# Relation-aware graph attention on one core: Q evicted by VectorE behind the sort, the one-hot cut by tile, gathers that begin before the edge phase is declared ready

## The chip, the core and the metric

The kernel runs on one core of a Trainium2 chip. The core has five engines with a program each: TensorE (PE in the profile; PEld is its weight load), VectorE (DVE), ScalarE (ACT), GpSimd (POOL) and SyncE (SP). They meet at semaphores. DMAs are issued by SP, ACT and POOL and run on 16 shared DMA engines; an indirect DMA (a gather of rows by an index column) is issued by GpSimd. The metric is device time in microseconds, lower is better.

## What is computed

Five relations, four heads of 64, N = 6250 nodes of 256 features, E = 100000 edges with a source, a destination and a relation each:

```python
Q = (jnp.einsum('nc,rch->rnh', x, Wq) + bq[:, None, :]).reshape(R, N, HEADS, OUT)
K = (jnp.einsum('nc,rch->rnh', x, Wk) + bk[:, None, :]).reshape(R, N, HEADS, OUT)
V = (jnp.einsum('nc,rch->rnh', x, Wv) + bv[:, None, :]).reshape(R, N, HEADS, OUT)
q_i = Q[edge_type, dst]
k_j = K[edge_type, src]
v_j = V[edge_type, src]
score = jnp.sum(q_i * k_j, axis=-1) * scale
seg = dst * R + edge_type
m = jax.ops.segment_max(score, seg, num_segments=N * R)
e = jnp.exp(score - m[seg])
s = jax.ops.segment_sum(e, seg, num_segments=N * R)
alpha = e / s[seg]
out = jax.ops.segment_sum(v_j * alpha[..., None], dst, num_segments=N)
...
x = _layernorm(x + out.reshape(N, HD) + bias, axis=-1)
```

Everything is float32. The edges are drawn at random and come unsorted.

## The kernel before

**Stage 1, projections and sort, side by side.** The nodes are 49 tiles of 128 rows (the last has 106). TensorE goes through 392 *chunks* (`for o in range(NO)`): first 147 chunks of Q, three per tile (512, 512 and 256 columns), then 245 of K and V, five per tile of 512 columns. A chunk is two matmuls, one per half of the 256 features; each fp32 matmul appears in the trace as two records. In a Q chunk a bf16 matmul with three rows (L544) puts the bias into the bank first. Chunk `o` uses bank `o % 4`, so it waits until chunk `o - 4` is evicted. ScalarE evicts all chunks below `OA` with a copy (L684), VectorE those from `OA` on with an addition of the bias (L967); before, `OA = NOQ = 147`, so VectorE evicts K and V. After chunk 0 of each Q tile TensorE transposes the next tile of x (L486). SP stores each finished Q tile to `q_tab` (L440), ScalarE's queue stores each K/V tile to `kv_tab` (L693).

Meanwhile VectorE sorts the edges by destination and relation with a bitonic network on a 128 x 1024 array of keys: 322 min/max entries of 512 columns (L855). Some layers need the array turned: TensorE transposes it (`turn_keys`, L498) and either VectorE reads it with a change of sign ("toT"), or ScalarE copies both halves back to SBUF (L715, "toR"); seven turns each way, and a last one. The places of the turns between chunks, `turn_at`, come from a small table of costs in units of one sort entry; `OS` is the first chunk behind the sort, 113 before. Then VectorE runs index steps 0 to 3 (`indices(step)`, L873 to L891), which give `kvidx` and, last, `qidx`; from chunk `OS` on it runs one step per chunk, each behind that chunk's eviction, if it has one (steps 4 to 14, `Z = OS - 4`).

With `qidx` there, GpSimd gathers 391 tiles of 128 query rows ahead of need (L373) into a ring of 14 slots `pq`, and SP stores them in order of use to `q_pre` (L431). Gather `j` below 49 needs the first `j + 1` tiles of Q in `q_tab`. SP's `keep_queries` comes four to a tile from tile `first = (OS + 2) // 3` on. From j = 72 on a gather also waits for a count of K/V evictions.

**Stage 2, edges.** 832 edge tiles of 128 edges, in 208 *superblocks* of four. GpSimd gathers K/V rows (L390) into a ring of 14 superblocks, and the 441 query tiles that were not prepared (L395); SP loads the 391 others from `q_pre` (L454). ScalarE lifts the queries to PSUM (L767), VectorE multiplies and reduces to scores (L987, L989), a softmax over segments follows once in eight superblocks, ScalarE scales V (L778), and 11 superblocks later TensorE sums by destination with a one-hot matrix (L608) that VectorE builds (L1036), and VectorE adds into `acc` (L1049). Before it all, `s_ready` must be given by VectorE (L981), which waits until everything of stage 1 is done, for the two stages share one region of SBUF.

**Stage 3** joins chunk borders, adds x and bias, and normalizes.

GpSimd's order between stage 1 and 2 is fixed by hand:

```python
pool.wait_ge(s_kvout[0], 16 * (NT // 2 + 2))
pool.wait_ge(s_kvout[1], 16 * (NT // 2))
pool.wait_ge(s_ready, 1)
for s in range(NSB):
```

## Time and profile before

| | us |
|---|---|
| median of 3 runs (lowest, highest) | 2569.26 (2567.68, 2575.88) |
| the profiled execution, its own time | 2567.08 |
| its span in the trace | 2565.3 |
| busy: TensorE / VectorE / ScalarE / GpSimd | 1631.4 / 1672.7 / 1222.1 / 1649.2 |

The profile page gives each engine's busy time, the span in 40 slices, the chain of work that ended last and the costliest groups of instructions. The groups have busy time, mean time of one, and the idle time of the engine just before them with what ended it; "issue" there means that nothing in the profile was waited for. The timeline lists instructions by start. Ends of matmuls are modelled. The granted TensorE clock is 1.00 up to 760 us and 0.5 to 0.7 from there on.

### The profile page before, as it was taken

How to read it: one execution, taken by the hardware profiler on the slowest of the kernel's cores; microseconds unless marked ns; L12 is line 12 of the kernel's file. 1: busy time of each engine (PE TensorE's matmuls, PEld its weight loads, DVE VectorE, ACT ScalarE, POOL GpSimd, SP SyncE). 2: the span in 40 equal slices, each digit the busy share in tenths (PEclk: the TensorE clock that was granted, in tenths of full speed). 3: DMA queues.
4: the chain of work that ended last, by engine and by line, in shares of the span. 5: the costliest groups of instructions: out<-in, count | busy, mean ns of one | idle time of the engine just before them, and what ended most of it. 6: DMA issues, size and time to landing. Idle time of an engine off the chain costs nothing.

```text
span 2565.3 us, 26061 instructions
## 1 busy us (share of the span) xinstructions
PE 1631.4 (64%) x5906; PEld 1128.7 (44%) x5906; DVE 1672.7 (65%) x3127; ACT 1222.1 (48%) x4159; POOL 1649.2 (64%) x1745
## 2 busy tenths in 40 slices
PE   7999999999990455545555555555544555555547
PEld 2444444444440344444444444444444444444435
DVE  8888333443435767777767777777767777777658
ACT  2333310000001666666666666666666666666656
POOL 1000557777776777777777777777777777777404
PEclk9999999999995555666665656666666566565675
DMA  5333789999998766666666666666666666666305
GB/s 185 123 117 117 245 292 363 363 362 364 363 360 295 222 195 200 195 197 200 199 198 199 197 200 199 198 199 199 197 196 199 197 199 201 199 199 199 109 11 174
DMA packets 285621, 553.28 MB, mean 216 GB/s; under 512 B 43605, under 2 KB 167719, under 8 KB 285466
## 3 DMA queue, kind: packets, MB, share of 16 engines
q0 software_dynamic: 106496, 327.26, 42.6%
q1 hardware_dynamic: 142836, 156.41, 18.4%
q10 hardware_dynamic: 36134, 67.94, 7.5%
q8 instruction: 48, 0.79, 0.1%
q14 instruction: 107, 0.88, 0.1%
HBM read 397.78 MB, written 153.65 MB: 215 GB/s over the span
## 4 chain that ended last, share of the span: by engine, by line
POOL 35%; PE 26%; issue 19%; ACT 7%; DVE 6%; DMA 6%; SPq 0%; DVEq 0%; POOLq 0%; ACTq 0%
POOL region L390 24%; PE sums L547 20%; POOL region L395 11%; ACT region L778 6%; DMA region<-q_tab,qidx 4%; PE sums L608 3%; DVE region L855 3%; PE sums L544 1%; DMA q_pre<-region 1%; DVE region L1127 1%; DVE region L1130 1%; ACT pairs L767 0%; DMA region<-kv_tab,kvidx 0%; POOL region L373 0%; DVE acc L1116 0%
## 5 line engine op out<-in xcount | busy, mean ns | idle before, releaser
L608 PE MATMUL sums<-region 128*128 128x130 f32 x3328 | 783.3, 420 | 787.3 <-ACT region L778 755.4
L608 PEld LDWEIGHTS sums<-region 128*128 128x128 f32 x3328 | 712.6, 320 | 845.0 <-ACT region L778 842.5
L390 POOL DMA_INDIRECT region<-kv_tab,kvidx x832 | 808.2, 971 | 261.9 <-issue 242.8
L778 ACT ACTIVATE region<-region 128x64 f32<-128x64 f32 x3328 | 821.5, 333 | 0.0
L547 PE MATMUL sums<-region,acc 128*128 128x512 f32 (+2 forms) x1568 | 673.7, 577 | 0.9 <-DVE region L967 0.9
L373 POOL DMA_INDIRECT region<-q_tab,qidx x391 | 371.9, 951 | 390.4 <-DVE qidx L891 249.8
L767 ACT COPY pairs<-region 128x1024 f32<-128x1024 f32 x208 | 211.4, 1016 | 792.4 <-DMA region<-kv_tab,kvidx 473.9
L1049 DVE TENSOR_TENSOR acc<-acc,sums 128x256 f32 x832 | 349.3, 420 | 327.9 <-PE sums L608 257.0
L395 POOL DMA_INDIRECT region<-q_tab,qidx x441 | 423.4, 960 | 134.4 <-issue 131.9
L547 PEld LDWEIGHTS sums<-region,acc 128*128 128x128 f32 (+1 forms) x1568 | 285.8, 190 | 314.1 <-issue 303.1
L967 DVE TENSOR_TENSOR region<-sums,region 128x512 f32<-128x512 f32 (+1 forms) x245 | 169.1, 691 | 301.0 <-PE sums L547 298.1
L987 DVE TENSOR_TENSOR pairs<-region,pairs 128x1024 f32<-128x1024 f32 x208 | 253.2, 1217 | 31.2 <-ACT pairs L767 31.0
L989 DVE TENSOR_REDUCE region<-pairs 128x16 f32<-128x1024 f32 x208 | 255.0, 1226 | 7.1
L855 DVE TENSOR_TENSOR region<-region 128x512 f32<-128x512 f32 x306 | 198.0, 689 | 19.6 <-ACT region L715 14.5
L684 ACT COPY region<-sums 128x512 f32<-128x512 f32 (+1 forms) x147 | 75.6, 514 | 213.9 <-PE sums L547 213.9
L1036 DVE TENSOR_TENSOR region<-iota_f,nrel 128x520 f32<-128x520 f32 x208 | 144.3, 694 | 0.0
L404 POOL TENSOR_TENSOR region<-region 128x256 f32<-128x256 f32 (+1 forms) x49 | 35.4, 729 | 117.8 <-DMA region<-in_x 117.6
L993 DVE TENSOR_TENSOR_SCAN region<-PEN,region 128x128 f32<-128x128 bf16 x52 | 24.2, 464 | 89.0 <-ACT region L750 70.5
L655 PE MATMUL sums<-ident,acc 128*128 128x128 f32 (+1 forms) x196 | 54.3, 435 | 27.8 <-DVE acc L1116 18.5
L729 ACT COPY region<-bank 1x512 f32<-1x512 f32 x52 | 29.4, 566 | 78.1 <-PE bank L568 78.1
L655 PEld LDWEIGHTS sums<-ident,acc 128*128 128x128 f32 (+1 forms) x196 | 42.3, 305 | 39.6 <-DVE region L1127 21.0
L544 PE MATMUL sums<-region 3*128 3x512 bf16 (+1 forms) x147 | 51.5, 350 | 9.0 <-DMA region<-region 9.0
(187 smaller groups left out, 783.0 us busy)
## 6 DMA issues: line engine op xcount, KB each, us to landing
kv_tab<-region ACTq DMA_DIRECT2D x48, 1280.0 KB, 7.5
q_pre<-region SPq DMA_DIRECT2D x391, 128.0 KB, 5.1
region<-q_pre SPq DMA_DIRECT2D x391, 128.0 KB, 3.5
q_tab<-region SPq DMA_DIRECT2D x48, 640.0 KB, 3.2
region<-q_tab,qidx POOLq DMA_INDIRECT x832, 3.7
region<-kv_tab,kvidx POOLq DMA_INDIRECT x832, 3.6
region<-in_x SPq DMA_DIRECT2D x96, 128.0 KB, 3.1
out<-region SPq DMA_DIRECT2D x48, 128.0 KB, 1.8
```

The lines of the kernel that those rows point to most:

```text
L373: pool.indirect_dma_start(pq[:, j % PQ, :], None, q_tab[0:min(stored * P, N) * R, :], bass.IndirectOffsetOnAxis(ap=qidx[:, PRE[j]:PRE[j] + ...
L390: pool.indirect_dma_start(ring[:, s % KS, i, :], None, kv_tab, bass.IndirectOffsetOnAxis(ap=kvidx[:, t:t + 1], axis=0)).then_inc(s_got[s % ...
L395: pool.indirect_dma_start(qring[:, s % QS, i, :], None, q_tab, bass.IndirectOffsetOnAxis(ap=qidx[:, t:t + 1], axis=0)).then_inc(s_got[s % ...
L547: done = nc.tensor.matmul(bank[o % 4][0:n, 0:w], acc[:, k, t * P:t * P + n], w_sb[:, k, :, :].rearrange("p u c -> p (u c)")[:, c0:c0 + w], ...
L608: done = nc.tensor.matmul(bank[i][:, h * W:(h + 1) * W], ring[:, q % KS, i, h * P:(h + 1) * P], oneh[:, q % 2, i, :], start=True, stop=True)
L767: nc.scalar.copy(qk, qring[:, s % QS, :, :]).then_inc(s_lift, 1)
L778: done = nc.scalar.activation(ring[:, q % KS, i, h * D:(h + 1) * D], ring[:, q % KS, i, C + h * D:C + (h + 1) * D], ACT.Copy, scale=alT[:, ...
L855: nc.vector.tensor_tensor(to[:, :, half, :], a[:, :, half, :], other_half, ALU.max if half else ALU.min).then_inc(s_sort, 1)
L967: nc.vector.tensor_tensor(stage[0:n, t % 2, c0:c0 + w], bank[o % 4][0:n, 0:w], b_sb[0:n, c0:c0 + w], ALU.add).then_inc(s_evD, 1)
L987: c(nc.vector.tensor_tensor(qk, ring[:, s % KS, :, 0:C], qk, ALU.mult))
L989: nc.vector.tensor_reduce(sc[:, (s // PERC) % 2, :, g:g + SB].rearrange("p h g -> p g h"), qk.rearrange("p i (h d) -> p i h d", h=H), AX.X ...
L1049: nc.vector.tensor_tensor(acc[:, :, bass.ds(at[i], P)], acc[:, :, bass.ds(at[i], P)], bank[i][:, 0:2 * W].rearrange("p (h n) -> p h n", h= ...
```

## The change

**Sort.** In a toR turn TensorE transposes the upper half first; ScalarE copies only that half, and VectorE's next two sort entries read the lower half from PSUM. The table of places counts nothing more for a toR turn; `OS` becomes 111, and most turns from the seventh on move one to two chunks forward.

**Queries first.** Index step 0 computes `qidx` in four operations, straight from the keys; what else steps 0 to 3 gave comes after it.

**Q evictions.** `OA` becomes 114: the chunks of Q tiles 38 to 48 (33 chunks) have no bias matmul, and VectorE evicts them with an addition of the bias row, held in `bq_sb`, which five more DMAs fill at the start.

**Handover.** GpSimd waits for `s_ready` only at superblock 3 (`FIRST`), since the first three ring slots lie where the weights were. The last K/V tile is stored relation by relation.

**One-hot.** Four `tensor_scalar` of 130 columns with a scalar column in place of one `tensor_tensor` of 520.

```diff
-                sort_at = turned + (2.5 if kind == "toR" else 0)
+                sort_at = turned
...
-    OA = NOQ
+    OA = QC * (OS // QC + 1)
...
+        bq_sb = stage[:, 1, 0:R * C]
...
+        FIRST = KC * UNITS * C // (SB * 2 * C)
...
-            return max(0, (j - EASE) * (NO - NOQ) // NPRE)
+            done = (j - EASE) * (NO - NOQ) // NPRE
+            return NOQ - OA + done if done > 0 else 0
...
-            pool.wait_ge(s_kvout[0], 16 * (NT // 2 + 2))
+            pool.wait_ge(s_kvout[0], 16 * (NT // 2 + 2 * R))
             pool.wait_ge(s_kvout[1], 16 * (NT // 2))
-            pool.wait_ge(s_ready, 1)
             for s in range(NSB):
+                if s == FIRST:
+
+                    pool.wait_ge(s_ready, 1)
...
+            for q in range(R):
+                sp.dma_start(bq_sb[:, q * C:(q + 1) * C], bq[q:q + 1, :].broadcast_to([P, C])).then_inc(s_bq, 16)
...
-                for half in range(2):
+                for half in (1, 0) if kind == "toR" else (0, 1):
...
-                    for half in range(2):
-                        act.wait_ge(s_turn, 2 * m + half + 1)
-                        nc.scalar.copy(keys[1 - TURNS[m][2]][:, half * 512:(half + 1) * 512], bank[5 + half][:]
-                                       ).then_inc(s_back, 1)
+                    act.wait_ge(s_turn, 2 * m + 1)
+                    nc.scalar.copy(keys[1 - TURNS[m][2]][:, 512:1024], bank[6][:]).then_inc(s_back, 1)
...
+            for r in range(R):
+                wait_evicted(act, NO - R + r)
+                for lo, hi in parts(NT - 1):
+                    act.dma_start(kv_rows[(NT - 1) * P + lo:(NT - 1) * P + hi, r, :],
+                                  stage[lo:hi, (NT - 1) % 2, r * CH:(r + 1) * CH]).then_inc(s_kvout[(NT - 1) % 2], 16)
...
+                    if back:
+
+                        dve.wait_ge(s_turn, 2 * back[0] + 2)
+                        dve.wait_ge(s_back, len([m for m in TURNS[0:back[0] + 1] if m[1] == "toR"]))
+                        one, other_half = bank[5][:].unsqueeze(1), a[:, :, 1, :]
...
+                    c.go(nc.vector.tensor_scalar(real[:], two[:, 0:TT, 0], float(DUMMY), None, ALU.is_lt))
...
+                    c(nc.vector.scalar_tensor_tensor(out=nrel[:], in0=two[:, 0:TT, 1], scalar=float(R - 8), in1=segi[:],
+                                                     op0=ALU.mult, op1=ALU.add))
+                    nc.vector.scalar_tensor_tensor(out=qidx[:], in0=nrel[:], scalar=float((8 - R) * HI), in1=real[:],
+                                                   op0=ALU.add, op1=ALU.mult).then_inc(s_qready, 1)
...
+                if OA <= o < NOQ:
+                    if o % QC == 0:
+                        dve.wait_ge(s_qout[t % 2], 16 * (t // 2))
+                    dve.wait_ge(s_proj, o + 1)
+                    q0 = c0 - 2 * R * C
+                    nc.vector.tensor_tensor(stage_q[0:n, t % 2, q0:q0 + w], bank[o % 4][0:n, 0:w],
+                                            bq_sb[0:n, q0:q0 + w], ALU.add).then_inc(s_evD, 1)
...
-                nc.vector.tensor_tensor(oneh[:, q % 2, :, :], iota_f[:].unsqueeze(1).broadcast_to([P, SB, W]),
-                                        nrel[:, q * SB:(q + 1) * SB].unsqueeze(2).broadcast_to([P, SB, W]),
-                                        ALU.is_equal).then_inc(s_oh, 1)
+                for i in range(SB):
+                    t = q * SB + i
+                    done = nc.vector.tensor_scalar(oneh[:, q % 2, i, :], iota_f[:], nrel[:, t:t + 1], None, ALU.is_equal)
+                done.then_inc(s_oh, 1)
```

On TensorE, behind the cast of index rows in Q tile 37 or 38 (L504 to L508 before, L514 to L518 in the change). Before:

```order
L505 MATMUL bank<-region 128x320
L508 MATMUL bank<-region 128x26 x4
L544 MATMUL sums<-region 128x512
L547 MATMUL sums<-region,acc 128x512 x2
L544 MATMUL sums<-region 128x256
L547 MATMUL sums<-region,acc 128x256 x2
L544 MATMUL sums<-region 128x512
L547 MATMUL sums<-region,acc 128x512 x2
L486 MATMUL pairs<-ident,region 128x128 x2
```

In the change:

```order
L515 MATMUL bank<-region 128x320
L518 MATMUL bank<-region 128x26 x4
L554 MATMUL sums<-region 128x256
L557 MATMUL sums<-region,acc 128x256 x2
L557 MATMUL sums<-region,acc 128x512 x2
L496 MATMUL pairs<-ident,region 128x128 x2
L557 MATMUL sums<-region,acc 128x512 x2
L525 MATMUL pairs<-region 128x512
```

The cast stands two chunks earlier in the program, and the one chunk after it is the last with a bias matmul (L554); before, all 147 had one.

On VectorE, from the cast's results on (L902 before, L922 in the change; `region` is most of SBUF). Before:

```order
L902 SCALAR_TENSOR_TENSOR region<-pairs,region 128x512 [waits s_cast,s_dve]
L904 SCALAR_TENSOR_TENSOR region<-bank,region 128x320
L908 TENSOR_SCALAR reci<-bank 1x52
L910 COPY recS<-bank 128x2x26
L916 TENSOR_TENSOR region<-region,recS 128x832 [waits s_dve,s_castc]
L917 TENSOR_TENSOR region<-region 128x832 [waits s_dve]
L920 TENSOR_TENSOR region<-region,recS 128x832 [waits s_dve]
L921 TENSOR_TENSOR region<-region 128x832 [waits s_dve]
```

In the change:

```order
L989 TENSOR_TENSOR region<-sums,region 128x512 [waits s_proj,s_qout0,s_dve]
L922 SCALAR_TENSOR_TENSOR region<-pairs,region 128x512 [waits s_cast]
L924 SCALAR_TENSOR_TENSOR region<-bank,region 128x320
L928 TENSOR_SCALAR reci<-bank 1x52
L930 COPY recS<-bank 128x2x26
L989 TENSOR_TENSOR region<-sums,region 128x512 [waits s_proj,s_dve,s_castc]
L936 TENSOR_TENSOR region<-region,recS 128x832
L937 TENSOR_TENSOR region<-region 128x832 [waits s_dve]
L989 TENSOR_TENSOR region<-sums,region 128x256 [waits s_proj,s_dve]
L940 TENSOR_TENSOR region<-region,recS 128x832
L941 TENSOR_TENSOR region<-region 128x832 [waits s_dve]
```

An eviction of a Q chunk (L989) now stands ahead of each index step.

On GpSimd, from the last query gather on (L373 and L390 before, L379 and L398 in the change). Before:

```order
L373 DMA region<-q_tab,qidx 128x256 [waits s_pqout12,s_evicted_dve]
L390 DMA region<-kv_tab,kvidx 128x512 [waits s_ready,s_kvout1,s_kvout0]
L390 DMA region<-kv_tab,kvidx 128x512 x11
L390 DMA region<-kv_tab,kvidx 128x512 [waits s_lifted]
L390 DMA region<-kv_tab,kvidx 128x512 x3
```

In the change:

```order
L379 DMA region<-q_tab,qidx 128x256 [waits s_pqout12,s_evicted_dve]
L398 DMA region<-kv_tab,kvidx 128x512 [waits s_kvout1,s_kvout0]
L398 DMA region<-kv_tab,kvidx 128x512 x11
L398 DMA region<-kv_tab,kvidx 128x512 [waits s_lifted,s_ready]
L398 DMA region<-kv_tab,kvidx 128x512 x3
```

The wait for `s_ready` has moved back by 12 gathers.

## Rows read from the trace of the kernel before

**Rows 1.** The page: its head, DMA busy in tenths by 40 slices, the chain by engine

```profile
span 2565.3 us, 26061 instructions
...
DMA  5333789999998766666666666666666666666305
...
POOL 35%; PE 26%; issue 19%; ACT 7%; DVE 6%; DMA 6%; SPq 0%; DVEq 0%; POOLq 0%; ACTq 0%
```

**Rows 2.** Groups, GpSimd, 783 to 2410 us: busy, mean of one | idle before

```profile
L390 POOL DMA_INDIRECT region<-kv_tab,kvidx x832 | 808.2, 971 | 261.9 <-issue 242.8 <-PE sums L608 9.1 <-DVE region L981 8.7
L395 POOL DMA_INDIRECT region<-q_tab,qidx x441 | 423.4, 960 | 134.4 <-issue 131.9 <-ACT pairs L767 2.4
```

**Rows 3.** Timeline, handover from query to K/V gathers: start, us, engine, line, operation

```profile
774.25 0.94 POOL L373 DMA_INDIRECT region<-q_tab,qidx  x1 [0.30 <-issue]
782.52 0.49 DVE L980 MEMSET region<- 1x516 f32 x1 [16.63 <-DMA q_pre<-region]
...
783.91 0.95 POOL L390 DMA_INDIRECT region<-kv_tab,kvidx  x1 [8.71 <-DVE region L981]
...
793.23 1.02 ACT L767 COPY pairs<-region 128x1024 f32<-128x1024 f32 x1 [448.01 <-DMA region<-kv_tab,kvidx]
```

**Rows 4.** Timeline, GpSimd, the last gather

```profile
2402.12 0.95 POOL L395 DMA_INDIRECT region<-q_tab,qidx  x1 [0.30 <-issue]
```

**Rows 5.** Timeline, GpSimd: gather 19, and the 48th and 49th query gathers

```profile
289.97 0.94 POOL L373 DMA_INDIRECT region<-q_tab,qidx  x1 [2.74 <-DMA q_pre<-region]
...
339.84 0.94 POOL L373 DMA_INDIRECT region<-q_tab,qidx  x1 [4.00 <-DMA q_tab<-region]
346.78 0.94 POOL L373 DMA_INDIRECT region<-q_tab,qidx  x1 [6.00 <-DMA q_tab<-region]
```

**Rows 6.** Timeline, TensorE: a Q tile's bias matmul to the next tile's, then K/V

```profile
239.69 0.38 PE L544 MATMUL sums<-region 3*128 3x512 bf16 x1
...
245.65 0.38 PE L544 MATMUL sums<-region 3*128 3x512 bf16 x1
...
739.68 25.48 PE L547 MATMUL sums<-region,acc 128*128 128x512 f32 x59
```

**Rows 7.** Timeline, VectorE's first and last operation for qidx, the first gather

```profile
254.18 0.59 DVE L874 CAST region<-region 128x832 f32<-128x832 uint16 x1
...
261.38 1.02 DVE L891 TENSOR_TENSOR qidx<-nrel,region 128x832 int32<-128x832 f32 x1
...
262.69 1.36 POOL L373 DMA_INDIRECT region<-q_tab,qidx  x1 [249.81 <-DVE qidx L891]
```

**Rows 8.** Timeline, the seventh toR turn; then VectorE's waits, 0 to 262 us

```profile
236.22 0.66 PE L498 MATMUL pairs<-ident,region 128*128 128x128 f32 x4 [0.80 <-DVE region L855]
...
236.91 0.58 ACT L715 COPY region<-pairs 128x512 f32<-128x512 f32 x1 [1.08 <-PE pairs L498]
...
238.09 3.35 DVE L855 TENSOR_TENSOR region<-region 128x512 f32<-128x512 f32 x5 [1.92 <-ACT region L715]
...
DVE region L855 <- ACT region L715: 14.5, 7, 2.8
```

**Rows 9.** Timeline, VectorE and GpSimd where they meet; L1008 alone; L841 alone

```profile
849.04 0.69 DVE L1036 TENSOR_TENSOR region<-iota_f,nrel 128x520 f32<-128x520 f32 x1
849.19 1.36 POOL L390 DMA_INDIRECT region<-kv_tab,kvidx  x1 [0.30 <-issue]
...
285.81 0.59 DVE L941 TENSOR_SCALAR nrel<-nrel 128x832 f32<-128x832 f32 x1
285.98 1.25 POOL L373 DMA_INDIRECT region<-q_tab,qidx  x1 [0.30 <-issue]
...
830.11 0.95 POOL L390 DMA_INDIRECT region<-kv_tab,kvidx  x1 [0.30 <-issue]
830.74 0.34 DVE L1008 TENSOR_SCALAR PEN<-XF 128x129 bf16<-128x129 bf16 x1
...
16.08 0.75 DVE L841 TENSOR_SCALAR region<-region 128x1024 f32<-128x1024 f32 x1
```

More of the change, by code:

```diff
@@ L117, in gnn_kernel @@
             OS = o
-    OA = NOQ
+    OA = QC * (OS // QC + 1)
     Z = OS - 4
-    assert OS < NOQ and Z + 15 + NCK + 4 < NO, Z
+    assert OA < NOQ and Z + 15 + NCK + 4 < NO, Z
     ctx = ExitStack()
@@ L196, in gnn_kernel @@
         ring = cut(KS * SB * 2 * C).rearrange("p (s i w) -> p s i w", s=KS, i=SB)
+        FIRST = KC * UNITS * C // (SB * 2 * C)
+        assert all(AHEAD[s] == SB for s in range(FIRST))
         qring = cut(QS * SB * C).rearrange("p (s i w) -> p s i w", s=QS, i=SB)
@@ L847, in sort_entry @@
                     dve.wait_ge(s_sort, e)
-                    dve.wait_ge(s_back, 2 * len([m for m in TURNS if m[1] == "toR" and m[0] <= e]))
                 if kind in ("flip", "half"):
@@ L887, in indices @@
                 if step == 3:
-                    c.go(nc.vector.tensor_tensor(kvidx[:], lof[:], real[:], ALU.mult))
-                    c(nc.vector.scalar_tensor_tensor(out=nrel[:], in0=nodef[:], scalar=float(R), in1=nrel[:],
-                                                     op0=ALU.mult, op1=ALU.add))
-                    nc.vector.tensor_tensor(qidx[:], nrel[:], real[:], ALU.mult).then_inc(s_qready, 1)
-                    dve.wait_ge(s_qready, 1)
+                    c(nc.vector.tensor_tensor(kvidx[:], lof[:], real[:], ALU.mult))
                 if step == 4:
```

25 lines of the change are left out of this document (13 added, 12 removed).

## The prediction

> **What bounds the kernel now.** I read the page's head and chain first, then GpSimd's groups and waits, then the timeline at the places where one stage hands over to the next. The chain that ended last [rows 1] is led by GpSimd's gathers (L390 and L395, 35%), and its "issue" share is the gap between them. In the edge phase GpSimd issues 832 + 441 = 1273 gathers without a real wait: the groups [rows 2] give 971 and 960 ns each, and the idle time before them, 261.9 + 134.4 us, is 0.30 us per gather but for some 14 us, 8.7 of them one wait for L981 at the very start. From the first at 783.91 [rows 3] to the last at 2402.12 [rows 4] that is 1618.2 us for 1272 pitches, 1.272 us each. An undisturbed gather takes 0.943 + 0.30, nearly 1.25 us. Behind the last gather comes a tail (2402 to 2565) that the change does not touch in anything that paces it.
>
> So the end moves by what the first edge gather gains, plus what the pitch gains. Going back from 783.91: GpSimd has issued the 391 query gathers one by one up to 774.25; from the 49th, at 346.78, they run at 427.47/342 = 1.250 us with no further wait [rows 3, 5]. That 49th gather waited 6.00 us for q_tab (the one before it 4.00): it needs the last tile of Q. It follows that **the end of the Q projections sets the gather stream, and the stream sets the end.** TensorE's K and V work is nearly parallel to it: its last eviction is at 765 and four of its chunks take some 1.72 us each [rows 6] (59 matmul records of a quarter chunk in 25.48 us), 245 chunks.
>
> **Part 1, 33 Q chunks without bias matmuls (tiles 38 to 48).** A tile with biases takes 245.65 - 239.69 = 5.96 us [rows 6]. Without them two chunks of 512 and one of 256 cost at K and V's rate 2.5 x 1.727 = 4.32, and the two transposes of x some 0.35: 4.67 us. A tile gains 1.29 us, 11 tiles 14.2 us. The lower end is the bias matmuls' own pitch alone, 0.3 us twice and 0.2, or 0.83 x 11 = 9.1 us; I take the K and V rate, since those are the same instructions. VectorE now evicts these chunks (0.7 us for 512 columns) between the index steps. Steps 8 to 14 are about two operations of 832 elements at 1.02 us per chunk [rows 7], so it falls behind: some 13 us of steps plus 4.3 us of evictions against 7 chunks of 1.6 us. TensorE may be four chunks ahead, which nearly covers it; it then waits for the flags that ScalarE turns into heads. I charge 1.5 us (0 to 4). The sort's shifts of place move turns between chunks and conserve TensorE's work. Net: Q ends **12.5 us earlier** (7 to 16), and so do the 49th gather and all behind it, since nothing behind it waits. K and V's last eviction comes as much earlier, near 753.
>
> **Part 2, sort and query rows first.** In a turn back (toR) VectorE stands from 236.17 to 238.09, 1.92 us, while TensorE transposes twice and ScalarE copies twice [rows 8]; the seven cost 14.5 us in the waits. Now only the second half is copied, beside the other half's transposes, so VectorE can go on 0.57 us sooner, when the first copy's slot ends: 4.0 us. The later "toT" turns, placed some chunks sooner, lose their two long waits but get small ones. Replaying the chunk table with these prices puts the last turn 3.8 us earlier. Then qidx: before, from the first index operation at 254.18 to the first gather at 262.69, 8.5 us; now two of 0.59, two of 1.02 and the semaphore gaps, 3.6 us. So the first gather comes about 8.7 us earlier, near 254. I cost this at nothing: gathers 15 to 48 wait for the ring of 14 slots, which SP empties four to a tile [rows 5] (the 2.74 us), and the 48th and 49th for Q's last tiles. If that cover were gone it would be worth up to 8.7 us; it isn't, since 48 gathers need 60 us and Q's end is 80 us away.
>
> **Part 3, the handover.** After the last query gather at 774.25 GpSimd now waits only for the K/V stores, not for the landing, the store to q_pre and VectorE's clearing (782.52), so the next gather can follow at 1.25 instead of 9.66 us [rows 3]: **8.4 us**. The K/V stores are issued by then with 8 us to spare, and the last is cut into five. What is late next: gather 13 waits for s_ready and the first lift. Ready comes 8.9 us after the last query gather, gather 13 would go 16.3 us after it; the lift needs four loads issued after ready and took until 10.1 us behind it (793.23), but then it waited for its K/V rows. I expect it at 15, so this fits by a hair. Bounds: 8.4, or 4 if the lift is as late as it was.
>
> **Part 4, one-hot by tile.** The trace shows what the old operation does to GpSimd. L1036 starts at 849.04 and takes 0.69; the gather of 849.19 takes 1.36 instead of 0.94: it ends 0.82 after L1036 does [rows 9]. A compare of two SBUF operands holds a gather's beginning. Counted over the timeline, 109 of the 1273 gathers began under L1036, the first at 849.19, and together lost 23.7 us of the 31 that [rows 2] hold over 943 ns. A tensor_scalar in fp32 does it too: L941 of 285.81, and the gather of 285.98 takes 1.25, again 0.82 behind its end. The other way round, L1008 began 0.63 us into a gather and took 0.34 us instead of 0.20 [rows 9]: a scalar operation also meets the second half of a gather. So four short ones have two windows per gather, but each holds it for its own length only. Length: L841 with a scalar from SBUF takes 0.75 us for 1024, L941 0.59 for 832; columns cost 1.06 ns between L1036 (520, 0.69) and L891 (832, 1.02) and half of that in a scalar operation, so 130 columns come to 0.28 from L841 and 0.22 from L941, against 0.20 for L1008's 129: I take 0.25. Four in a row: 0.7 to 1.0 us in VectorE's superblock of 7.8 us, hidden, as VectorE is idle for over 2 us in each. Mean hold per superblock for random starts: before 0.69^2/2/1.27 = 0.19 us; now 4 x 0.25^2/2/1.27 = 0.10 in one window, up to 0.20 in both. That is 0 to 50% less than 23.7 us if the gather gets in between two of them. Bounds: all 24 us gained (no hold at all), or 25 us lost (the four act as one hold of 1 us in one window and a half). I take a gain of **2 us**.
>
> The Trainium skill (VectorE: DVE Perf Modes, "The TRN2 errata — SBUF-src ops pay a fixed extra latency per instruction") speaks against cutting one operation in four: a fixed cost is paid each time, and it advises 512 elements or more. By its formula four would take an estimated 0.51 us against 0.60 for one, as the halved rate pays for the fixed parts; the one took 0.69 here, and the four are not in this trace.
>
> **Sum** against the profiled execution's 2567.08 us: -12.5 - 8.4 - 2 = -22.9, so 2544.2. The median of the runs is 2.2 us higher: **2546.5**. A measurement here can tell 0.3%, 7.7 us, so faster means below 2561.5.
>
> **Rivals.**
> - *The one-hot gives its 24 us back whole* (10%): for it, that the scalar operand leaves VectorE's second read free; against it L941. 2524.
> - *The holds double* (16%): both windows are hit and the four act as one. Loss 15 to 25 us, time 2563 to 2572 at the far end, 2558 at the near one with a gain of Q at its upper bound. For it: operations without a wait between them follow at once.
> - *GpSimd is stopped by every scalar operation, wherever in the gather it falls* (5%). 832 operations x 0.25 us x 0.75 (a gather's share of its pitch) = 156 us more, less 23.7 and 21: 2680. It turns slower once a single operation costs GpSimd more than (21 + 24)/832 = 54 ns. For it: the first gather of all, which met two such operations and took 1.36 [rows 7]. Against it: L1008 lay within a gather of 0.95 us that was not longer [rows 9]. The Trainium skill (SBUF — State Buffer, "SBUF: two separate sides") states this rule: an operation in a 2-port mode takes the pair of ports as an exclusive lock, and GpSimd cannot write descriptors meanwhile; at a gather's beginning the trace agrees (0.82 us after the end, twice).
> - *Part 1 is eaten up* (9%): VectorE's evictions behind index steps hold TensorE for 8 us or more, Q ends 5 us earlier only: 2554.
> - *Nothing moves* (4%), because the transfers of the K/V phase, at nine tenths or more in all its slices [rows 1], pace the gathers and not their issue: against it the pitch of 1.250 us, the same as elsewhere.
>
> **Numbers.** Forecast as summed: 56%. The range 2525 to 2566 holds forecast, the eaten-up case, most of the first and of the doubled holds; outside stay the 5%, the far ends. Faster by over 0.3%: 0.85, within: 0.09, slower: 0.06.
>
> **What would show it.** First query gather near 254 and still waits of some us at the 48th and 49th, the 49th near 334; no wait after it; last one near 762; first K/V gather 1.25 us later; gather 13 with 0 to 2 us of wait; GpSimd's means near 0.965 in the edge phase; a tile of Q without biases at 4.7 to 5.3 us. I am wrong if the edge pitch is over 1.29 us, if K/V's last store lands after the last query gather, or if the tail behind the last gather changes from 163 us by more than 2.

## The result, and the profile after

The changed kernel takes 2540.77 us (median of 4 runs, 2539.55 to 2540.99), the kernel before 2572.17 in the same comparison (4 runs, 2567.68 to 2575.88): a ratio of 0.9865, 95% interval 0.9851 to 0.9878. The profiled execution took 2540.96 us against 2567.08, 26.1 us less. The forecast of 2546.5 was 5.7 us too high, its range held the time, and its sign was right. Its parts were not: two of the four terms were wrong by far, in opposite directions, as the traces show below.

The page of the changed kernel: head, DMA busy in tenths, the chain that ended last by engine (against [rows 1]).

```profile
span 2539.1 us, 26489 instructions
...
DMA  6333789999999766666666666666666666666305
...
POOL 33%; PE 26%; issue 16%; ACT 9%; DVE 9%; DMA 6%; SPq 0%; DVEq 0%; ACTq 0%; POOLq 0%
```

The groups of GpSimd and VectorE in the edge phase (against [rows 2]: 971 and 960 ns).

```profile
L398 POOL DMA_INDIRECT region<-kv_tab,kvidx x832 | 794.7, 955 | 255.3 <-issue 245.4 <-PE sums L618 7.0 <-ACT pairs L780 2.8
L403 POOL DMA_INDIRECT region<-q_tab,qidx x441 | 420.2, 953 | 134.5 <-issue 132.3 <-ACT pairs L780 2.1
...
L1066 DVE TENSOR_SCALAR region<-iota_f,nrel 128x130 f32<-128x130 f32 x832 | 186.2, 303 | 0.0
```

The timeline of the changed kernel at the places of [rows 3, 4, 5, 7]: start, us, engine, line, operation, idle before.

```profile
257.19 1.47 POOL L379 DMA_INDIRECT region<-q_tab,qidx  x1 [244.29 <-DMA q_tab<-region]
...
337.01 0.95 POOL L379 DMA_INDIRECT region<-q_tab,qidx  x1 [4.27 <-DMA q_tab<-region]
343.27 0.95 POOL L379 DMA_INDIRECT region<-q_tab,qidx  x1 [5.31 <-DMA q_tab<-region]
...
771.74 0.95 POOL L379 DMA_INDIRECT region<-q_tab,qidx  x1 [0.30 <-issue]
772.99 0.94 POOL L398 DMA_INDIRECT region<-kv_tab,kvidx  x1 [0.31 <-issue]
780.07 0.49 DVE L1008 MEMSET region<- 1x516 f32 x1 [18.72 <-DMA q_pre<-region]
787.84 1.02 ACT L780 COPY pairs<-region 128x1024 f32<-128x1024 f32 x1 [449.67 <-DMA region<-q_pre]
789.60 0.95 POOL L398 DMA_INDIRECT region<-kv_tab,kvidx  x1 [1.90 <-ACT pairs L780]
...
2376.36 0.95 POOL L403 DMA_INDIRECT region<-q_tab,qidx  x1 [0.30 <-issue]
```

Laid beside the rows of before, these marks divide the 26.1 us:

| stretch | before | after | difference | forecast |
|---|---|---|---|---|
| 49th query gather (end of Q) | 346.78 | 343.27 | -3.5 | -12.5 |
| 49th to last query gather | 427.47 | 428.47 | +1.0 | 0 |
| last query to first K/V gather | 9.66 | 1.25 | -8.4 | -8.4 |
| first to last gather of the edge phase | 1618.2 | 1603.4 | -14.8 | -2, and 0 to +2 at gather 13 |
| behind the last gather | 163.1 | 162.8 | -0.4 | 0 |

Q's end moved by a quarter of what was forecast, and the edge phase by seven times as much.

### The profile page after: what moved, and what is told of

Its sections match the earlier page's. It is cut to its first block, busy times and chain, and to the rows that moved or that the text cites. A ratio compares the mean times of both kernels' runs of the same rounds, so it can differ in the third digit from the quotient of the medians.

```text
span 2539.1 us, 26489 instructions
## 1 busy us (share of the span) xinstructions
PE 1619.8 (64%) x5873; PEld 1124.9 (44%) x5873; DVE 1729.1 (68%) x3784; ACT 1205.2 (47%) x4119; POOL 1633.8 (64%) x1745
## 4 chain that ended last, share of the span: by engine, by line
POOL 33%; PE 26%; issue 16%; ACT 9%; DVE 9%; DMA 6%; SPq 0%; DVEq 0%; ACTq 0%; POOLq 0%
POOL region L398 22%; PE sums L557 20%; POOL region L403 10%; ACT region L791 8%; DVE region L873 5%; DMA region<-q_tab,qidx 4%; PE sums L618 3%; DMA q_pre<-region 1%; ACT pairs L780 1%; PE sums L554 1%; DVE region L1156 1%; DVE region L1159 1%; DMA region<-in_x 0%; DVE acc L1078 0%; DVE acc L1145 0%
## 5 line engine op out<-in xcount | busy, mean ns | idle before, releaser
L398 POOL DMA_INDIRECT region<-kv_tab,kvidx x832 | 794.7, 955 | 255.3 <-issue 245.4
L379 POOL DMA_INDIRECT region<-q_tab,qidx x391 | 373.1, 954 | 386.7 <-DMA q_tab<-region 258.3
L873 DVE TENSOR_TENSOR region<-region 128x512 f32<-128x512 f32 x292 | 189.0, 689 | 5.1
L1066 DVE TENSOR_SCALAR region<-iota_f,nrel 128x130 f32<-128x130 f32 x832 | 186.2, 303 | 0.0
L694 ACT COPY region<-sums 128x512 f32<-128x512 f32 (+1 forms) x114 | 58.7, 515 | 181.4 <-PE sums L557 181.4
L598 PE MATMUL bank<-ident,region 128*128 128x128 f32 x26 | 11.0, 421 | 61.2 <-DVE region L1017 61.2
```

The source lines that it names most:

```text
L379: pool.indirect_dma_start(pq[:, j % PQ, :], None, q_tab[0:min(stored * P, N) * R, :], bass.IndirectOffsetOnAxis(ap=qidx[:, PRE[j]:PRE[j] + ...
L398: pool.indirect_dma_start(ring[:, s % KS, i, :], None, kv_tab, bass.IndirectOffsetOnAxis(ap=kvidx[:, t:t + 1], axis=0)).then_inc(s_got[s % ...
L873: nc.vector.tensor_tensor(to[:, :, half, :], one, other_half, ALU.max if half else ALU.min).then_inc(s_sort, 1)
L1066: done = nc.vector.tensor_scalar(oneh[:, q % 2, i, :], iota_f[:], nrel[:, t:t + 1], None, ALU.is_equal)
```

## The experiments

Three questions follow. Is the edge phase's gain the one-hot's, and is it the *kind* of operation (a scalar operand leaves VectorE's second read free) or the *length* of one operation that decides? Is Q's end late because VectorE's evictions lag behind the index steps (the rival "eaten up"), because of the heads' flags, which ride along with the same chunks, or because of TensorE's clock? And what is the handover worth once what comes behind it is counted? In the expectations "E" stands for the theory that TensorE's clock falls after its long standing idle before the first turn, and "G" for the theory that a slightly slower gather belongs to the chip and not to the program.

The marks of all traces, in us. "Idle" is TensorE's wait just before the first turn, "clock" what it was granted from 91 to 96 us, "held" the time by which the 1273 gathers of the edge phase exceed the median gather of their own trace, added up. That median is 949 ns in the changed kernel and 946 in the nine others, so 3.8 us of the changed kernel's edge phase are not in its "held". The four kernels of the last series are told of at their place.

| kernel | idle, clock | 49th query gather | last query gather | first K/V gather | last gather | edge phase | held |
|---|---|---|---|---|---|---|---|
| before | 1.41, 1.00 | 346.78 | 774.25 | 783.91 | 2402.12 | 1618.2 | 27.4 |
| changed | 2.27, 0.50 | 343.27 | 771.74 | 772.99 | 2376.36 | 1603.4 | 6.8 |
| e1_whole_onehot | 1.99, 0.66 | 341.86 | 769.42 | 771.03 | 2392.58 | 1621.5 | 29.1 |
| e2_only_onehot | 2.29, 0.50 | 350.20 | 777.82 | 788.24 | 2384.14 | 1595.9 | 5.1 |
| e3_onehot_tile_tt | 3.62, 0.66 | 342.26 | 769.84 | 771.09 | 2376.86 | 1605.8 | 12.3 |
| e4_ready_first | 1.89, 0.70 | 341.35 | 768.86 | 776.57 | 2373.56 | 1597.0 | 6.2 |
| e5_no_q_evict | 1.81, 1.00 | 347.08 | 774.56 | 775.81 | 2376.93 | 1601.1 | 7.0 |
| e6_late_flags | 2.83, 1.00 | 334.25 | 761.84 | 771.97 | 2368.79 | 1596.8 | 6.0 |
| e7_turn0_later | 0.99, 1.00 | 340.65 | 768.14 | 769.39 | 2370.05 | 1600.7 | 7.3 |
| e10_before_turn0 | 0.14, 1.00 | 347.80 | 775.36 | 785.49 | 2403.03 | 1617.5 | 26.8 |

The runs were made in series, each with runs of the kernel before beside it (the expectations call a series a "call"). Times are best compared within a series, as the kernel before itself had medians of 2572.17, 2569.11 (e1, e2, e3, e6) and 2569.27 us (e4, e5, e7, e10) in the three of this table. The changed kernel was in the first alone.

### e1_whole_onehot: all of the change but the one-hot

```diff
-                for i in range(SB):
-                    t = q * SB + i
-                    done = nc.vector.tensor_scalar(oneh[:, q % 2, i, :], iota_f[:], nrel[:, t:t + 1], None, ALU.is_equal)
-                done.then_inc(s_oh, 1)
+                nc.vector.tensor_tensor(oneh[:, q % 2, :, :], iota_f[:].unsqueeze(1).broadcast_to([P, SB, W]),
+                                        nrel[:, q * SB:(q + 1) * SB].unsqueeze(2).broadcast_to([P, SB, W]),
+                                        ALU.is_equal).then_inc(s_oh, 1)
```

> The changed kernel with the one-hot built by one tensor_tensor of 520 columns again. Theory A (short holds): a gather that begins under a VectorE operation waits for the end of that one operation only, so four operations of 0.28 us hold GpSimd far less than one of 0.69. Then the mean of an edge gather goes back from 955/953 ns to 971/960, the edge phase gets 15 to 17 us longer, and the time is 2556 to 2558. Rival B (the phase itself moved): the gathers became shorter because the edge phase starts in another rhythm, not because of the one-hot; then the means stay near 955 and the time stays within 3 us of 2541.

Measured: 2558.67 us (2555.11 to 2564.19), ratio to before 0.9962 (0.9951 to 0.9973). GpSimd's groups in the edge phase:

```profile
L398 POOL DMA_INDIRECT region<-kv_tab,kvidx x832 | 808.3, 972 | 255.4 <-issue 238.5 <-PE sums L618 12.8 <-ACT pairs L780 3.5
L403 POOL DMA_INDIRECT region<-q_tab,qidx x441 | 425.1, 964 | 134.3 <-issue 133.7 <-ACT pairs L780 0.6
```

The gathers are back at 972 and 964 ns, those of [rows 2], and the edge phase at 1621.5 us. The other three parts together are worth 0.4%; the greater part of the gain is the one-hot's.

### e2_only_onehot: the kernel before with the one-hot alone

The same edit the other way round, on the kernel before.

> The kernel before with the one-hot by tile alone. Theory A: 14 to 17 us faster than before, about 2555, with edge gathers at 953 to 956 ns. Rival B: within 3 us of before.

Measured: 2547.80 us (2546.79 to 2550.14), ratio 0.9918 (0.9902 to 0.9935).

```profile
L390 POOL DMA_INDIRECT region<-kv_tab,kvidx x832 | 790.9, 951 | 262.6 <-issue 242.8 <-DVE region L981 9.5 <-PE sums L608 7.9
L395 POOL DMA_INDIRECT region<-q_tab,qidx x441 | 418.4, 949 | 134.4 <-issue 132.5 <-ACT pairs L767 1.8
```

From 971 and 960 to 951 and 949 ns: the edge phase is 22.3 us shorter (1595.9 against 1618.2) with nothing else changed in it, and the time that gathers are held falls from 27.4 to 5.1 us. The expectation, read from the changed kernel's trace, had 14 to 17 us; the gain by the median is 21. The one-hot alone gives what e1 takes away (18.1 us, and the 3.8 of the median gather).

### e3_onehot_tile_tt: four short operations of the old kind

```diff
-                    done = nc.vector.tensor_scalar(oneh[:, q % 2, i, :], iota_f[:], nrel[:, t:t + 1], None, ALU.is_equal)
+                    done = nc.vector.tensor_tensor(oneh[:, q % 2, i, :], iota_f[:],
+                                                   nrel[:, t:t + 1].broadcast_to([P, W]), ALU.is_equal)
```

> The changed kernel with the one-hot by tile, but by four tensor_tensor of 130 columns instead of four tensor_scalar. If the length of the single operation decides, gathers keep 953 to 957 ns and the time stays within 2 us of the changed kernel (2541). If it is the kind (the scalar operand frees VectorE's second read), each of the four still holds like a quarter of the old one but they act as one hold of 0.7 to 1.0 us: gathers at 965 to 975 ns and 2553 to 2565.

Measured: 2541.41 us (2540.17 to 2541.89), ratio 0.9891 (0.9874 to 0.9907). The source view gives, for one line, min/median/max in ns, first and last start. In e3:

```profile
L1066 DVE TENSOR_TENSOR region<-iota_f,nrel x832: 256/286/355, 839.0 to 2437.3; 128x130 f32<-128x130 f32 x167
```

and in the changed kernel:

```profile
L1066 DVE TENSOR_SCALAR region<-iota_f,nrel x832: 252/281/520, 839.6 to 2436.4; 128x130 f32<-128x130 f32 x167
```

One operation takes 286 against 281 ns, and the mean gathers are nearly the same (957 and 953 ns against 955 and 953). But the changed kernel's median gather is the longer one. Held above their own median are 12.3 us in e3 and 5.1 to 7.3 in the six kernels of the table with the scalar form; e3's edge phase is 1605.8 us with 2.95 us at gather 13, that of e7 and e5 1600.7 and 1601.1 with 2.84 and 3.61. So most of the gain is the *length* of one operation (27.4 to 12.3, some 15 us), and the *kind* is worth some 5 us more, which the nearly equal run times hide. The expectation's two cases leave this one out. How the hold ends is seen in the changed kernel's timeline, VectorE and GpSimd:

```profile
839.57 0.87 DVE L1066 TENSOR_SCALAR region<-iota_f,nrel 128x130 f32<-128x130 f32 x4
...
839.85 1.01 POOL L398 DMA_INDIRECT region<-kv_tab,kvidx  x1 [0.31 <-issue]
```

The gather begins inside the row of four, which still has 0.59 us to go. By the rule of [rows 9], an end 0.82 us behind the operation's, it would have ended 1.41 us after its start had the four been one; it took 1.01, and its end is 0.82 us behind that of the second of the four (840.05). It was held by that one and got in ahead of the next. Counted from the starts and ends in the traces, 128 gathers began under the old one-hot and lost 23.4 us above the median (the forecast counted 109, and 23.7 us over 943 ns); under the four of the changed kernel 158 began and lost 2.4, under the four of e3 158, with 6.9. In all three the held ones end 0.81 to 0.83 us behind an operation.

In a gather's second half it is VectorE that waits: the short scalar operations that begin 0.50 to 0.60 us into a gather took mostly 500 down to 400 ns in place of 281, so that they end about 1.00 us behind the gather's start (the 520 ns above began at 0.48), and the gathers are not longer by it. Those that begin in its first 0.4 us are not slowed. The tensor_tensor form, at most 355 ns, is nearly free of that.

### e5_no_q_evict: the change with Q evicted as before

```diff
-    OA = QC * (OS // QC + 1)
+    OA = NOQ
```

> The changed kernel with OA = NOQ: ScalarE evicts all of Q again, and every Q chunk has its bias matmul; the half copy of the sort, the early qidx, the handover and the one-hot stay. Theory C: Q ends 6 to 8 us later (the 49th query gather at 349 to 351 instead of 343), the time is 2547 to 2549. By the prediction's own size of this part (12.5 us) it would be 2553; if K/V and not Q set the gather stream it would be within 2 us of 2541.

Measured: 2541.00 us (2538.96 to 2542.65), ratio 0.9889 (0.9872 to 0.9906). Its 49th gather starts at 347.08, that of before at 346.78 [rows 5]: the quicker sort and the earlier `qidx` give nothing at Q's end, so Part 2 is indeed covered. Against e7 below (340.65, the same granted clock) the 33 chunks are worth 6.4 us at the 49th gather, or 7.2 without the 0.8 us by which e7's own edit has Q late already at 245 us; between e2 (350.20) and the changed kernel (343.27), both at 0.50, 6.9 us. Forecast: 12.5. The expectation missed e5's time by 6 us (2547 to 2549): it was worked out from the changed kernel's trace, with its fallen clock and its gathers of 949 ns, and e5 has neither. In the same series e7 is 7.9 us below e5.

### e6_late_flags: the heads' flags moved behind Q

TensorE's flag transposes (L534, L535), ScalarE's copies and VectorE's last index steps move from chunks 120 to 145 into K and V's chunks, which have no bias matmul either.

```diff
+    X0 = NOQ
...
-                if Z + 13 <= o < Z + 13 + NCK:
-                    turn_same(o - Z - 13)
+                if X0 <= o < X0 + NCK:
+                    turn_same(o - X0)
...
-                indices(o - Z)
+                if o - Z < 15:
+                    indices(o - Z)
+                if o > X0 + NCK:
+                    indices(o - X0 + 13)
```

> The changed kernel with the 26 pairs of flag transposes (L534, L535) moved from the Q chunks 120 to 145 to the K/V chunks from 147 on. Theory C (why tiles of Q without bias gained 0.61 us and not 1.29): TensorE drains at every change between chunk matmuls and something else, and the flag transposes between the chunks keep that cost where the bias matmuls went. Then a Q tile without either takes 4.5 to 4.7 us instead of 5.88, Q ends 10 to 12 us earlier (the 49th query gather near 332 instead of 343), and since K/V then still ends where it did, 761, the last query gather (760) meets the K/V stores: the first K/V gather comes 5 to 9 us earlier and the time is 2532 to 2536. Rival D (VectorE's evictions pace the tiles): the tile stays over 5.3 us and the time within 3 us of 2541.

Measured: 2532.78 us (2529.37 to 2533.70), ratio 0.9854 (0.9838 to 0.9871): faster than the kernel before, and in the same series 8.6 us below e3, the change but for the one-hot's form. Against the changed kernel itself it isn't clear: 8.0 us by the medians of two series, but the ratios to before, 0.9854 and 0.9865, lie in each other's intervals. A tile of Q on TensorE, from one transpose of x to the next, first in the changed kernel:

```profile
311.81 0.38 PE L496 MATMUL pairs<-ident,region 128*128 128x128 f32 x2
312.03 0.27 PE L534 MATMUL pairs<-ident,region 128*128 128x128 f32 x1
312.23 0.22 PE L535 MATMUL pairs<-ident,region 1*128 1x1 f32 x1
312.38 1.98 PE L557 MATMUL sums<-region,acc 128*128 128x512 f32 x4
...
317.69 0.38 PE L496 MATMUL pairs<-ident,region 128*128 128x128 f32 x2
```

and in e6:

```profile
298.83 0.38 PE L497 MATMUL pairs<-ident,region 128*128 128x128 f32 x2
299.05 4.46 PE L558 MATMUL sums<-region,acc 128*128 128x512 f32 x12
303.35 0.38 PE L497 MATMUL pairs<-ident,region 128*128 128x128 f32 x2
```

5.88 us with flags, 4.52 without. The forecast had 4.67 for a tile without biases, near enough for a tile that nothing else interrupts. But 9 of the 11 tiles also carry flags, and a tile with biases *and* flags took 6.49 us in the kernel before: where the flags are, dropping the biases gains 0.61 us a tile and not 1.29. (That TensorE "drains" at such a change, as the expectation has it, no row shows; the rows show only the times.) Of the waits that the forecast had charged, the changed kernel's Q had two, 0.85 us for ScalarE at the first flag and 0.17 for VectorE.

That e6 has the 49th gather at 334.25, where the forecast had it "near 334", is in part chance, for its Q lost time in two other ways: TensorE stood 3.8 us for VectorE's evictions of Q, the longer time while VectorE itself waited 6.86 us for the store of an earlier Q tile, and behind that the granted clock was 0.50 for a while (waits; timeline of TensorE and VectorE; windows row, with 0.50 behind the five busy times).

```profile
PE sums L558 <- DVE region L990: 3.8, 2, 2.7
...
319.21 1.62 DVE L990 TENSOR_TENSOR region<-sums,region 128x512 f32<-128x512 f32 x3 [6.86 <-DMA q_tab<-region]
...
319.96 10.55 PE L558 MATMUL sums<-region,acc 128*128 128x512 f32 x24 [2.71 <-DVE region L990]
...
321.00:324.40 3.40, 3.40 (x8) 1.96 (x7) 1.29 (x2) 0.00 (x0) 2.48 (x4) 0.50 0.86 293
```

Of the 9.0 us that Q's end gains on the changed kernel, nearly all is lost again at the handover:

```profile
761.84 0.95 POOL L380 DMA_INDIRECT region<-q_tab,qidx  x1 [0.30 <-issue]
762.36 0.69 DVE L996 TENSOR_TENSOR region<-sums,region 106x512 f32<-106x512 f32 x1 [1.03 <-PE sums L558]
...
771.97 0.94 POOL L399 DMA_INDIRECT region<-kv_tab,kvidx  x1 [9.18 <-DMA kv_tab<-region]
```

The last eviction of K and V (762.36) now comes behind the last query gather (761.84), and the first K/V gather waits 9.18 us for the last tile's stores to issue and land. Part 3's gain needs K and V to end some 9 us ahead of the query gathers. What e6 keeps comes in the edge phase, 1596.8 us against 1603.4: by gather 13 the lift is done, and its undisturbed gather is 946 and not 949 ns. The second of these, 3.8 us, can't be put down to the flags (see the last series).

### e4_ready_first: the wait for ready back in its old place

```diff
-                if s == FIRST:
+                if s == 0:
```

> The changed kernel with GpSimd's wait for s_ready back before the first K/V gather. Theory A: the first K/V gather comes 8.4 us later again (9.7 us behind the last query gather) and gather 13 loses its 1.6 us wait for the lift, so the time is 6 to 8 us longer than the changed kernel: 2547 to 2549. Rival B: the edge phase makes up for a late start elsewhere (its consumers, not GpSimd's stream, set the end); then under 3 us longer.

Measured: 2539.19 us (2537.58 to 2541.20), ratio 0.9887 (0.9871 to 0.9904), where 2547 to 2549 was expected. The handover in e4:

```profile
768.86 0.95 POOL L379 DMA_INDIRECT region<-q_tab,qidx  x1 [0.30 <-issue]
775.18 0.49 DVE L1008 MEMSET region<- 1x516 f32 x1 [15.77 <-DMA q_pre<-region]
776.57 0.94 POOL L398 DMA_INDIRECT region<-kv_tab,kvidx  x1 [6.77 <-DVE region L1009]
```

Its gap is 7.7 us and not the 9.66 of before (why ready comes 2 us sooner behind the last query gather here, no run tells). Its edge phase is 1597.0 us against 1600.7 and 1601.1 in e7 and e5, which have the early start: starting 6.5 us sooner costs 3.7 to 4.1 us later, 2.5 to 3.3 of it the wait for the lift at gather 13. Net, moving the wait is worth 2.4 to 2.8 us in these traces. From before's gap it is 8.4 less some 4, near the lower bound that the forecast named ("4 if the lift is as late as it was"). That e4's time isn't above the changed kernel's has two small reasons: its granted clock at the first turn was 0.70 against 0.50, and its undisturbed gather takes 946 ns against 949.

### e7_turn0_later and e10_before_turn0: TensorE's clock at the first turn

Before the sort's first turn (L508) TensorE waits for VectorE. In the changed kernel, the timeline row of that turn and the windows row of 91 to 96 us (busy, granted clock, DMA share, GB/s):

```profile
90.29 1.11 PE L508 MATMUL pairs<-ident,region 128*128 128x128 f32 x4 [2.27 <-DVE region L873]
...
91.00:96.00 5.00, 5.00 (x11) 0.50 0.10 35
```

and in e7, whose only edit is to put the first two turns one chunk later (`turn_at[33], turn_at[34] = 0, 1`, where they stood at 32 and 33; L510 here is L508 there):

```profile
91.23 0.66 PE L510 MATMUL pairs<-ident,region 128*128 128x128 f32 x4 [0.99 <-DVE region L875]
...
91.00:96.00 5.00, 4.72 (x23) 1.00 0.08 27
```

> The changed kernel with its first two turns one chunk later (33 and 34 instead of 32 and 33). In the changed kernel's trace TensorE stood 2.3 us before its first turn and the granted clock was 0.50 of full speed from 91 to 96 us, 3.3 us lost; in e2, whose first stage is that of the kernel before, it was the same, while e6 stood 2.8 us and kept its clock. Theory E: the standing brings the drop, not always; with no standing at that turn the clock stays at 1.00, the 49th query gather comes 3 us earlier (340), and the median is 2 to 4 us below the changed kernel, with less spread. Rival F: the drop comes whatever TensorE does around 90 us; then it is there in this trace too and the time stays within 1.5 us.

Measured, e7: 2533.14 us (2532.33 to 2533.44), ratio 0.9861 (0.9844 to 0.9877): 7.9 us below e5 and 6.1 below e4 of the same series, and against the changed kernel as unclear as e6 (ratios 0.9861 and 0.9865). The changed kernel stood 2.27 us and was granted 0.50 (1.2 GHz) for 6.8 us, from 90.3 to 97.1, so that four transposes took 1.11 us and not 0.66; e7 stood 0.99 us and kept 1.00 (2.4 GHz). The 49th gather comes 2.6 us sooner. That is all of the 7.9 us between the two traces that the clock can explain: 3.7 more come in the query gathers behind it and the edge phase, by the median gather of 946 in place of 949 ns above all, and 1.6 in the tail.

> The kernel before with its first two turns one chunk later, and nothing else. Theory E: no drop of the clock at 91 us in its trace, runs within 2565 to 2569, its median 1 to 4 us below before's (whose runs so far go from 2566 to 2576). Rival F: the same spread as before and the same median within 1 us.

Measured, e10 (the same move on the kernel before): 2569.54 us (2565.47 to 2573.72, 12 runs), ratio 1.0001 (0.9993 to 1.001): nothing. The kernel before kept 1.00 in its trace in any case, and the move itself delays Q by about 1 us (347.80 against 346.78). Theory E holds in part: the rows show the loss where the clock fell, but not that every long stand makes it fall. e6 stood 2.83 us there and kept 1.00, e5 1.81; e2, whose first stage is that of before, got 0.50 in its trace where before had 1.00. Taken with the traces of the last series below, the clock fell at this turn in 8 of the 11 traces with the turn in its old place (stands of 1.89 to 3.97 us; the three that kept it stood 1.41, 1.81 and 2.83), and in none of the 3 with the move (e7, e10, e9: 0.99 us or less).

### The last series: e13_again, e12_old_sort, e11_unsplit, e9_best

e13 is the changed kernel unedited; e12 takes the sort's turn-back and the index steps back to the kernel before; e11 is e6 with the last K/V tile stored whole (`store_kv(NT - 1)`); e9 is e11 with e7's edit.

> The changed kernel once more, unedited, on one chip with the other kernels of this call. In its first trace an undisturbed gather took 949 ns with a gap of 306, in all other traces 946 and 305, and the 342 query gathers behind the 49th took 428.5 us instead of 427.5. Theory G: that was the chip of that call, not the change; then this trace shows 946 again, the edge phase is 4 us shorter (1599 to 1600) and the median is 2535 to 2538. Rival H: the change itself does it; then 949 and 2540 to 2541 again.

> The changed kernel with the sort's turns back, their table and the index steps of the kernel before (OA is 114 all the same). Theory A (the prediction's: this part is hidden): the first query gather comes 4 to 9 us later, near 262, the 49th where it was within 2 us, and the time is within 2.5 us of the changed kernel in the same call. Rival: the ring of 14 and SP's stores pass the delay on; then the 49th comes 4 us or more later and the time with it.

> e6 (flag transposes in the K/V chunks) with the last K/V tile stored whole, in two DMAs instead of ten. In e6 the first K/V gather stood 9.2 us for the K/V stores: the last eviction was at 762.4, the last of ten stores was issued at 767.3. Theory I: the ten issues are what is late; two DMAs issued at 763 land at 768 to 770, the first K/V gather comes 2 to 4 us earlier than in e6 (968 to 970 behind by two digits: 768 to 770), and the time falls by 1 to 3 us, if the lift does not take it back. Rival J: the bytes are late behind the q_pre stores, not the issues; then 771 to 773 again and the time as e6 within 1 us.

> e11 with the first two turns one chunk later as in e7: flags late, last tile whole, no standing before the first turn. By addition it gains over e11 what the granted clock lost there in those runs (0 to 3 us, none if e11's trace shows 1.00 at 91 us), so 2528 to 2533; K/V's end is then again what the first K/V gather waits for. If a gain at Q's end no longer counts, as the last query gather now waits for the K/V stores, it is within 1 us of e11.

Measured in this series: before 2965.85 us (35 runs, 2956.85 to 2983.73), e13 2973.43, e12 2971.54, e11 2967.11, e9 2966.11; ratios 1.0016 (0.9999 to 1.0032), 1.002 (1.0005 to 1.0035), 1.0002 (0.9987 to 1.0018), 0.9999 (0.9987 to 1.0011). Every kernel, before too, was some 400 us longer than in the series ahead of it. The windows of 400 to 760 us and of the edge phase (busy of PE, PEld, DVE, ACT, POOL; granted clock, DMA share, GB/s) in e13:

```profile
400.00:760.00 360.00, 287.54 (x583) 119.52 (x584) 99.75 (x149) 0.00 (x0) 231.54 (x245) 0.87 0.84 284
940.00:2810.00 1870.00, 787.28 (x3470) 708.82 (x3470) 1164.92 (x2674) 1024.20 (x3565) 1213.34 (x1270) 0.60 0.59 175
```

and in the changed kernel's first trace:

```profile
400.00:760.00 360.00, 360.00 (x840) 159.02 (x839) 145.15 (x210) 0.00 (x0) 272.49 (x288) 1.00 1.02 362
775.00:2376.00 1601.00, 787.71 (x3470) 709.38 (x3470) 1179.13 (x2685) 1016.18 (x3566) 1212.18 (x1271) 0.62 0.70 205
```

The engines do the same work (GpSimd 1213 us of gathers in both edge phases), but 284 GB/s were moved in the K/V phase against 362, and 175 against 205 in the edge phase. Timeline and waits of e13, GpSimd (waits: us in total, times, longest):

```profile
936.83 0.95 POOL L398 DMA_INDIRECT region<-kv_tab,kvidx  x1 [76.28 <-DMA kv_tab<-region]
...
POOL region L398 <- remote: 216.7, 73, 9.6
POOL region L398 <- PE sums L618: 89.9, 48, 2.4
```

GpSimd waits 76 us for K/V's stores at the handover and, beyond the 0.30 us between any two gathers, some 270 us in the edge phase, where the changed kernel had 1.5, the lift at gather 13. Transfers set the pace, and in that condition no part of the change is worth anything: that is the rival "nothing moves", true under other conditions than those it was forecast for. What slowed the transfers isn't known; this series ran on another chip than the series of e1 to e10, so chip and time can't be told apart. Whether e6's and e7's gains add, whether the unsplit store helps, and the price of the sort's part stay open in the usual condition. One thing this series settles is theory G, which falls: of four programs run one after the other on the same chip, e13 and e9 have a median gather of 949 ns, e12 and e11 of 946, and the changed kernel has 949 in both of its traces. It seems to go with the program, on one trace of each other kernel; by what, no run tells. Over 1273 + 342 gathers its 3 ns are about 5 us.

## Why the prediction was right or wrong

- **What bounds the kernel: right.** GpSimd's stream ran from the 49th query gather to the end at 1.25 us with no other wait than gather 13's, and the tail behind the last gather was 162.8 us (forecast 163 within 2).
- **Part 1, mis-sized: 12.5 us forecast, 6.4 to 7.2 measured.** The failing step is "A tile gains 1.29 us, 11 tiles 14.2 us". It counted only bias matmuls and took every tile as one without flags. 9 of 11 tiles carry flag transposes between their chunks; there the gain is 0.61 us, and 9 x 0.61 + 2 x 1.44 (5.96 less 4.52) = 8.4, less the waits of 1.0 us, is close to what the runs show. e6 gets to the forecast figure by taking the flags out, with 3.8 us of waits and a fallen clock against it. The rival "eaten up" came near in size (5 us) but by another mechanism: the waits cost 1.0 us (0.85 + 0.17) where 1.5 was charged and that rival had 8 us or more.
- **A term that was missing: the clock.** In the profiled execution some 3.4 us went to TensorE at 0.50 behind the first turn (half of 6.8), so only 3.5 of the 6.9 us are left in its 49th gather. The first turn was nowhere in the forecast.
- **Part 2: right that it is hidden, and right in size where the clock held.** First query gather at 257.19, forecast 254. `qidx` took 3.5 us (253.69 to 257.19) as forecast. The turn back saved 0.46 us and not 0.57:

```profile
235.95 0.66 PE L508 MATMUL bank<-ident,region 128*128 128x128 f32 x4 [0.58 <-DVE region L873]
...
236.65 0.59 ACT L724 COPY region<-bank 128x512 f32<-128x512 f32 x1 [0.54 <-PE bank L508]
...
237.36 1.29 DVE L873 TENSOR_TENSOR region<-pairs,region 128x512 f32<-128x512 f32 x2 [1.46 <-ACT region L724]
```

  VectorE's gap is 1.46 us against 1.92 [rows 8], but the turn at 98 us had one of 3.98, because of the clock, and the first index operation came 0.5 us sooner (253.69 against 254.18), not 3.8. In the traces without a fallen clock there, the first gather is at 253.85, 253.95 and 254.61 (e5, e6, e7), so the forecast's 3.8 us and its 254 hold. None of it reaches Q's end, as e5 shows.
- **Part 3: right at the gap, too high in its net.** 1.25 us as forecast. Ready came 8.9 us and the lift 16.1 us behind the last query gather, and gather 13 waited 1.90 us where 0 to 2 was forecast; with more holds and waits behind it, some 4 of the 8.4 us came back in the edge phase.
- **Part 4, mis-sized: 2 us forecast, 22.3 measured (e2).** The failing step is "Mean hold per superblock for random starts ... up to 0.20 in both". It charged the full length of each short operation, and up to twice. A gather's second half costs GpSimd nothing, as VectorE's operation is the one that waits, and at its beginning a held gather gets in between two of the four. The formula also leaves out what its own rows show: a held gather ends 0.82 us behind the operation and a free one takes 0.946, so the last 0.13 us of an operation hold nothing, a fifth of one of 0.69 us but nearly half of one of 0.28. Without that term it gives 0.19 x 208 = 39 us for the kernel before, where 23.7 were counted; with it, 26. The evidence against "gains all" was L941 holding a gather: true, but it lasts 0.59 us, where one short operation lasts 0.28. So the rival "gives its 24 us back whole", at 10%, was nearly the truth in its size; of its reason, the scalar operand, e3 leaves some 5 us. "The holds double" and "stopped by every scalar operation" fell. On the last, the Trainium skill (SBUF — State Buffer, "SBUF: two separate sides") has GpSimd unable to write descriptors while a 2-port operation holds the pair of ports. The trace agrees at a gather's beginning, and only for the operation in progress; in the gather's second half it is VectorE's operation that waits, with 0.40 to 0.50 us for 0.28, and in between neither does.
- **VectorE's own price.** Four take 0.87 us and one took 0.69 [rows 9]; forecast 0.7 to 1.0, hidden. The Trainium skill (VectorE: DVE Perf Modes, "The TRN2 errata — SBUF-src ops pay a fixed extra latency per instruction") advises against short operations, and the trace agrees that four cost VectorE more, 0.18 us here. It doesn't decide, since VectorE isn't the bound.
- **Sum.** The edge phase gave 14.8 and not 22.3 us because of the lift (1.6), the gather of 949 and not 946 ns (3.8), and 2.1 of other waits and holds. Against the forecast, Q's end and the query gathers behind it fell short by 10.0 us and the edge phase gained 12.8 more. That Q's shortfall of 9 us and the one-hot's excess cancelled is luck; the forecast total was closer than its reasons.

## What to carry to other kernels

Where GpSimd's gathers are the bound, keep each of VectorE's single operations short: a 0.69 us operation cut in four of 0.28 us gave 22 us over 1273 gathers, some 15 of them with the old kind of operation too. When costing work taken out of a stretch, look at what else lies in that stretch: dropping the bias matmuls gave 1.4 us a tile only where no other small matmuls cut the chunks apart, and 0.6 elsewhere. And an earlier start is worth what is left of it at the next gate; follow the gain to that gate (here the lift, or the K/V stores in e6) before adding it up.

## What was not expected of the hardware

- TensorE's stand before the first turn and the clock granted behind it varied between traces of the same first stage (1.41 us and 1.00 in before, 2.29 us and 0.50 in e2), and a longer stand kept 1.00 (2.83 us in e6). About 3.4 us hang on it. Putting the turn one chunk later kept 1.00 in all three traces that have it.
- Undisturbed gathers take 946 or 949 ns, as it seems by program.
- A whole series ran at 284 GB/s where the series ahead of it had 362, with all kernels 15 to 17% longer; a comparison made then would have called this change worthless (1.0016).
